# Two layer graph network on one core: layer two's loads get a DRAM side of outermost size four

## What is computed

```python
msg_in = jnp.concatenate([x[row], x[col]], axis=-1)
messages = jax.nn.relu(msg_in @ W_msg + b_msg)
aggregated = jax.ops.segment_sum(messages, col, num_segments=x.shape[0])
h = jax.nn.relu(jnp.concatenate([x, aggregated], axis=-1) @ W_upd + b_upd)
mu = jnp.mean(h, axis=-1, keepdims=True)
var = jnp.mean(jnp.square(h - mu), axis=-1, keepdims=True)
return (h - mu) * jax.lax.rsqrt(var + LN_EPS) * gamma + beta
...
x = _layernorm(x + _L0_gnn_ref(x, src, dst, edge_weight, ...), axis=-1)
x = _layernorm(x + _L1_gnn_ref(x, edge_index, ...), axis=-1)
```

## Time and profile before

| What | Value |
|---|---|
| Runs (3), median | 4035.39 us (4032.98 to 4035.66) |
| The profiled execution: its own time, which is its span | 4403.8 us |
| TensorE busy (share of the span) | 3810.6 us (87%) |
| VectorE busy | 3380.9 us (77%) |
| ScalarE busy | 2779.1 us (63%) |
| GpSimd busy | 2477.9 us (56%) |
| Bytes moved by the DMA engines | 707.82 MB, mean 161 GB/s |
| q0, the gathers of GpSimd | 359.18 MB, 29.2% of 16 engines' span |
| q1, the transfers of SyncE | 343.13 MB, 23.1% |
| Chain of waits, by engine | PE 44%, DVE 29%, issue 11%, not named 9% |

### The profile page before, as it was taken

The page is one execution under the profiler, slowest core; times in us unless marked ns, Lnnn a source line. Parts: engine busy times, 40 slices in busy tenths (PEclk is TensorE's granted clock), DMA queues, the critical chain, the costliest instruction groups (busy, mean ns, idle before and its releaser), DMA issues.

```text
span 4403.8 us, 85804 instructions
## 1 busy us (share of the span) xinstructions
PE 3810.6 (87%) x26341; PEld 3176.6 (72%) x26341; DVE 3380.9 (77%) x7638; ACT 2779.1 (63%) x7247; POOL 2477.9 (56%) x2585
## 2 busy tenths in 40 slices
PE   4999999899999999956888888878888888888886
PEld 4999999788888888845666666666666666666665
DVE  7999999799999999955666666666666666666666
ACT  4888888777777777744555555555555555555554
POOL 2653655344455555536666666666666666666662
PEclk8999999999999999988899999999999989999998
DMA  5776544567777777743444444444444444444442
GB/s 133 243 231 226 190 189 188 197 191 206 209 209 209 209 209 208 206 141 110 127 142 129 136 127 140 132 130 136 131 132 136 135 131 131 128 129 139 131 131 72
DMA packets 344434, 707.82 MB, mean 161 GB/s; under 512 B 58153, under 2 KB 201334, under 8 KB 343954
## 3 DMA queue, kind: packets, MB, share of 16 engines
q0 software_dynamic: 114912, 359.18, 29.2%
q1 hardware_dynamic: 229074, 343.13, 23.1%
HBM read 507.96 MB, written 195.74 MB: 160 GB/s over the span
## 4 chain that ended last, share of the span: by engine, by line
PE 44%; DVE 29%; issue 11%; another core or an unknown queue 9%; ACT 2%; DVEq 2%; DMA 2%; SPq 1%; POOL 0%; ACTq 0%; POOLq 0%
PE ps L1327 11%; PE ps L1339 10%; DVE big L1903 7%; PE ps L1157 6%; DVE scr L1753 4%; PE ps L1305 4%; DVE arena L1913 3%; DVE arena L1756 3%; PE ps L1219 2%; PE ps L1164 2%; PE ps L1230 2%; PE ps L1188 2%; DVE scr L1756 1%; PE ps L1147 1%
## 5 line engine op out<-in xcount | busy, mean ns | idle before, releaser
L795 POOL DMA_INDIRECT arena<-d_p,tabs x1612 | 1543.0, 957 | 890.8 <-issue 457.3
L1913 DVE TENSOR_TENSOR arena<-arena,ps 128x512 f32<-128x512 f32 x806 | 527.0, 683 | 760.9 <-remote 503.8
L1327 PE MATMUL ps<-arena 128*128 128x256 f32 x3224 | 897.3, 419 | 240.1 <-DVE big L1903 174.2
L1111 ACT ACTIVATE arena<-arena 128x1024 f32<-128x1024 f32 x403 | 425.7, 1056 | 1004.8 <-DVE arena L1913 956.3
L1339 PE MATMUL ps<-big,scr 128*128 x3224 | 840.3, 401 | 219.6 <-DVE arena L1913 134.4
L1327 PEld LDWEIGHTS ps<-arena 128*128 128x128 f32 x3224 | 627.7, 205 | 424.2 <-ACT arena L1111 192.3
L1339 PEld LDWEIGHTS ps<-big,scr 128*128 128x128 f32 x3224 | 641.9, 202 | 356.9 <-issue 261.1
L1903 DVE SCALAR_TENSOR_TENSOR big<-big,tabs,ps 128x256 f32 x1612 | 767.8, 476 | 105.7 <-DVE big L1903 47.7
L781 POOL DMA_INDIRECT arena<-d_m,scr x392 | 531.2, 1355 | 564.0 <-DVE arena L1756 220.8
L1305 PE MATMUL ps<-arena,scr 128*128 128x256 f32 x2620 | 614.9, 384 | 10.5 <-DVE arena L1756 10.3
L1305 PEld LDWEIGHTS ps<-arena,scr 128*128 128x128 f32 x2620 | 483.7, 190 | 93.2 <-issue 32.9
(11 more groups left out here) (285 smaller groups left out, 5753.3 us busy)
## 6 DMA issues: line engine op xcount, KB each, us to landing
d_m<-arena SPq DMA_DIRECT2D x108, 603.0 KB
arena<-d_loc SPq DMA_DIRECT2D x135, 384.0 KB
d_m<-arena SPq DMA_DIRECT2D x108, 402.0 KB
arena<-d_p,tabs POOLq DMA_INDIRECT x1612
arena<-in_xT_dram SPq DMA_DIRECT2D x96, 256.0 KB
d_xp<-arena SPq DMA_DIRECT2D x49, 256.0 KB, 3.3
arena<-d_xp SPq DMA_DIRECT2D x49, 256.0 KB
d_x<-arena SPq DMA_DIRECT2D x49, 256.0 KB
```

The costliest lines, as they stand in the source:

```text
L795: e.indirect_dma_start(out=G1[j % 8][:, k, :], out_offset=None, in_=d_p, in_offset=bass.IndirectOffsetOnAxis(ap=tabS[:, j, k:k + 1], axis= ...
L1111: e.activation(G1[g % 8], G1[g % 8], ACT.Relu).then_inc(S("f_re"), 1)
L1327: m = e.matmul(turn(H, AB)[:, k * 256:k * 256 + 256], OH1[(j - 2) % 4][:, 2 * h + k, :], G1[(j - 2) % 8][:, 2 * h + k, :], start=True, sto ...
L1913: e.tensor_tensor(v, v, q2(turn(2 * j + h, QB)[:, :]), ALU.add).then_inc(S("f_m"), 1)
```

## The change

The residual rows get a tensor of their own, `d_xr`, and it and `d_y` are laid out in four quarters: quarter q holds, for every pair, the data of partitions 32q to 32q + 31. A view `quarters(t, p)` of a pair has the sizes 4, 32 and 512 in DRAM. The two stores in layer one and the three loads in layer two use it. The load of target numbers reads the same 3072 bytes for every partition, and its DRAM side goes from sizes 128 and 1536 with a step of 0 to 4, 32 and 1536 with steps of 0 and 0. The SBUF side is 128 partitions in all of them, and bytes and buffers are the same. A residual row is now moved as 2048 bytes in one piece where it was two pieces of 1024. The wait ahead of the load at o == 0 in layer one counts the residual stores issued so far (`kept`) instead of p - 1: the same number for pairs 0 to 46, one more for 47 and 48.

```diff
+        d_xr = dram("d_xr", (4, NP * 32, 512))
...
-        d_y = dram("d_y", (NP * 128, 512))
+        d_y = dram("d_y", (4, NP * 32, 512))
...
+        def quarters(t, p):
+
+            return t[:, p * 32:(p + 1) * 32, :]
+
...
+            kept = 0
...
-                        waitn(e, "b_s1", 16 * (p - 1))
+                        waitn(e, "b_s1", 16 * kept)
...
-                        e.dma_start(pair(d_x1, p), X1[p % 2]).then_inc(S("b_s1"), 16)
+                        kept += 1
+                        e.dma_start(quarters(d_xr, p), X1[p % 2].rearrange("p a b -> p (a b)")).then_inc(S("b_s1"), 16)
...
-                        e.dma_start(d_y[p * 128:(p + 1) * 128, :], XT1.rearrange("p a b -> p (a b)")).then_inc(S("b_s4"), 16)
+                        e.dma_start(quarters(d_y, p), XT1.rearrange("p a b -> p (a b)")).then_inc(S("b_s4"), 16)
...
-                e.dma_start(LBC[n % 2], d_loc[4 * BL * n:4 * BL * (n + 1), :].rearrange("(o a) b -> o (a b)", o=1).to_broadcast([128, BL * 512]))\
+                e.dma_start(LBC[n % 2], d_loc[4 * BL * n:4 * BL * (n + 1), :].rearrange("(o t a) b -> o t (a b)", o=1, t=1).to_broadcast([4, 32, BL * 512]))\
...
-                        e.dma_start(XTL[p % 2].rearrange("p a b -> p (a b)"), d_y[p * 128:(p + 1) * 128, :]).then_inc(S(f"g_in{p % 2}"), 16)
+                        e.dma_start(XTL[p % 2].rearrange("p a b -> p (a b)"), quarters(d_y, p)).then_inc(S(f"g_in{p % 2}"), 16)
...
-                            e.dma_start(XTQ.rearrange("p a b -> p (a b)"), d_y[(p + QL) * 128:(p + QL + 1) * 128, :]).then_inc(S("g_xq"), 16)
+                            e.dma_start(XTQ.rearrange("p a b -> p (a b)"), quarters(d_y, p + QL)).then_inc(S("g_xq"), 16)
...
-                        e.dma_start(XR, pair(d_x1, p)).then_inc(S("g_x"), 16)
+                        e.dma_start(XR.rearrange("p a b -> p (a b)"), quarters(d_xr, p)).then_inc(S("g_x"), 16)
```

## The result

The change takes **4084.18 us** (median of 4 runs, 4078.42 to 4090.19) against 4034.18 for the kernel before in the same comparison: 50.0 us more, ratio 1.0122, interval 1.011 to 1.0134. The forecast was 4063.0 us, slower, in a range of 4025 to 4140. So the direction and the range hold, and the size is 21 us short.

What follows compares the result with a forecast made beforehand. VectorE was taken to set layer one's pace, and GpSimd's gather issuing nearly to bound layer two. Layer one 18, between layers 7.1 and end 2.4 gave 27.5 us on 4035.4: 4063 us, range 4025 to 4140.

Steps and rivals of the forecast that it cites:

- Four engines: Changed transfers: outermost size 4 means four DMA engines, so 256 KB needs 3.20 us instead of 0.80.
- 0.4 us lost: Layer one, steady: gather delayed 4.76 us against 4.4 us of cover, loss over 45 pairs, 18 us.
- 92% instead of 71%: Layer one, steady: share of a 22.1 us pair that the four engines are busy, 20.4 us.
- From layer one to layer two, +7.1: Between the layers: late stores ahead of the load of x, and slower first target numbers, +7.1 us together.
- Layer two, 0: Layer two, steady: slower loads stay hidden because their users wait much longer anyway, 0 us.
- four full engines: Rival: in layer two loads and gathers fill four engines, slower loads make them the bound, 4196 us; chance 0.05.
- loads out of the way: Rival: weaker bursts on four engines shorten VectorE's unnamed waits in layer two, 3995 us; chance 0.14.
- The end, +2.4: End of layer two: TensorE waits longer for the last load of transposed rows, +2.4 us.
- 368.4 us of it belong to the profile's execution alone: Layer two: the gap between profiled 4403.8 and run 4035.4 us was put down to the profile's execution.
- hidden: Rival: still 16 engines (4035 us), or layer one keeps its cover and only edges cost (4045); chance 0.29.
- The signs named beforehand: Profile after: longer waits at layer two's start, at the end and in layer one; q1 share 13 to 14%.

Runs made afterwards that it cites:

- e3: The change with eighths in place of quarters, outermost size eight everywhere: 4408.79 us, ratio 1.0054 against the kernel before.
- e4: The change with halves in place of quarters, outermost size two everywhere: 4520.11 us, ratio 1.0314 against the kernel before.
- e9: The change with sixteenths in place of quarters, outermost size 16 everywhere: 4415.9 us, ratio 1.0032 against the kernel before.
- e6: The kernel before with residual rows in their own tensor as 128 rows of 2048 bytes, outermost size 128: 4036.22 us, ratio 0.9999.
- e8: The change itself run again, on a second chip of the quicker kind: 4083.73 us, ratio 1.0112 against the kernel before.
- e7: The kernel before with only the transposed rows in quarters (their store and both loads): 4064.89 us, ratio 1.0065.
- e12: The kernel before, unchanged, run again for its profile on a chip of the slower kind: 4401.39 us.
- e1: The change with each residual and transposed store of layer one as four transfers of 32 partitions: 4407.87 us, ratio 1.0058 against the kernel before.
- e11: The same kernel as e1 on another chip of the slower kind: 4435.44 us, ratio 1.0081 against the kernel before.
- e10: The kernel before with only the residual rows in quarters (store, load and the count in the wait): 4408.56 us, ratio 1.0016.
- e5: The kernel before with outermost size four in the 135 loads of target numbers alone: 4039.79 us, ratio 1.0006.

## Why the prediction was right, and where its sizes were off

**Four engines** (the change to a transfer): right, by e3, e4, e9 and the raises of the semaphores. The estimate of 3.20 us for 256 KB is near 4 x 0.62 = 2.5; the 20.6 kB per us from the queue's share was too low for an undisturbed load.

**"0.4 us lost" in layer one, 18 us in all**: right in its mechanism, too small. The measured term is 0.46 to 0.73 us a pair over 44 pairs and 4.6 and 4.2 us outside them, 24.8 and 36.1 us against e6. I priced one gather, that of 1106.45, with a cover of 4.4 us against a delay of 4.76 from both stores. By its record it had landed at 1111.33, so the cover was 1.71 + 1.98 = 3.7 us. In the change it lands 2.7 to 3.1 us later in the median, and only in some pairs later than the cover: it costs VectorE 0.23 us a pair in the first profile and 0.15 in e8. So the 0.4 was near for this gather, by luck, with cover and delay both too large. What the sum left out are the gathers behind it, above all the next one (0.41 and 0.21 us a pair), then the third (0.07 and 0.06). Together that is 0.72 and 0.42 us, near all of the loss of 0.73 and 0.46. Nor are the stores equal, as I had them: alone, the transposed one costs 0.31 us, nearly all at the gather that I had priced (e7), the residual one nothing (e10). That VectorE loses what is left after the cover, and nothing of the rest, is as predicted: its waits grew by 27 us (25.4 and 7.6 where it had 6.0), those of ScalarE for gathers by 112 (201.8 where it had 89.8).

**"92% instead of 71%"**: too high. By the same count halves would bring 71% + 11.2/22.1 = 122%, a pair of some 27 us; e4's pair took 22.97. So such shares can't be added up to how full an engine is.

**From layer one to layer two, +7.1**: measured 7.5 and 7.8 against e6 (40.3 us). Both profiles of before from the slower kind have 38.4 us there, against which it would be 9.4 and 9.7; which is the right base isn't settled. Of its parts, the landing of x is +2.4 (2.9 predicted), the first target numbers +3.56 (3.6).

**Layer two, 0**: 4.2 and 4.8 us on the quicker kind, 1 us for each 100 groups. The gap of GpSimd stayed:

```profile
3000.11 0.95 POOL L802 DMA_INDIRECT arena<-d_p,tabs  x1 [0.31 <-issue]
```

So the rival of four full engines (4196) is out, and so is the one of loads out of the way (3995): VectorE's unnamed waits of 467.2 us are not in the change's list on the quicker kind (there it waits for gathers, 367.1 us, and 337.3 in e6), and on the slower one they are waits for TensorE (e12) and are there with loads on four engines too (469.3 us in e1).

**The end, +2.4**: TensorE's wait grew by 2.54, the stretch behind the last message by 3.6 to 3.8. The 2.54 are right by luck in part: 1.8 of it is engines (16 to 4), 0.8 is what e9 has with all 16.

**"368.4 us of it belong to the profile's execution alone"**: wrong. It is the chip (e12), and within layer two it is time in which the other engines wait for TensorE. The inference drawn from it, that layer two is near GpSimd's issuing in a run, holds for the runs on the quicker kind only. Had the change been timed on the slower kind, the loads of layer two, put down at 0, would have been the second term (16 us in e11).

**The rival "hidden", 4045**: it would have been near for e10's part of the change alone. By the Trainium skill ("DMA: Bandwidth & Descriptors", section "Queues, rings and completion order") an engine takes turns between its queues, packet by packet; from that alone I had worked out that layer one loses nothing. Here layer one lost 25 to 36 us, and e1 got them back with the same bytes over 16 engines. Turns between queues don't keep a gather from being late when four of its sixteen shares take turns with a store: those four came 1.4 to 2.4 us after the other twelve in e8.

**The signs named beforehand** all came: VectorE's wait at layer two's start went from 14.61 to 19.53 us (about 18 said), TensorE's at the end from 3.52 to 6.06, ScalarE's for gathers from 67.3 to 144.3, VectorE's new waits are 27 us over some 50 pairs, and the share of q1 in layer two hardly moved (15.0% in 2200:4000, 15.7% in e6).

What wasn't settled: why a pair takes 22.67 us in one execution and 22.94 in another, why the transposed store lands 4.4 us later and not 2.4, and why TensorE's results come late in layer two on the slower kind of chip. No experiment beat the kernel before; e6 equals it.

## What to carry to other kernels

Look at the outermost size of a direct transfer in DRAM: with 128 partitions on the other side, sizes 2, 4, 8 and 16 were the number of DMA engines that it got here. Count the raises of its semaphore in the trace to see it. A small one costs little where the transfer has long cover (e5 nothing that can be told, e10 0.2%), and costs where a gather that everybody waits for shares its engines (e7), and at every place where a load is on the path, here start and end. Price each store by every gather that is under way with it or behind it, and not by one; undo it alone, and don't add up two delays: the cover is taken off first.

Before laying a trace beside the times of a kernel, see that its span is one of theirs. Where it isn't, don't give the difference to the profile, and compare no row of a stretch whose pace differs.

## What the runs showed of the hardware that was not expected

- Two kinds of chip, or states of one, for one kernel: 4036 against 4384 and 4402 us, all of it in layer two (5.09 against 6.0 us a group), with layer one the same to 0.01 us a pair. The granted clock was 0.977 against 0.943 on average. TensorE is busy 3813.6 us in e12 and 3705.3 in e6, so the clock could carry 108 of 369 us at most; VectorE's and GpSimd's instructions are as long, and their added waits end on TensorE's semaphores, over 1 us after any recorded end of a matmul that raises them (e12).
- The time of a load grew by T, 2T and 4T (0.62, 1.15 and 2.66 us) as its outermost size went 16, 8, 4, 2, and by 0.8 us from 128 to 16 (in one run, e9), where all sixteen raises of the semaphore are there in both.
- Halves cost layer one hardly more than quarters (22.97 against 22.67 to 22.94 us a pair), eighths next to nothing (22.25 against 22.22).
- A store of 256 KB on four engines beside the gathers landed 2.4 us later in one place and 4.4 us later 2.3 us further on (e10, e7).
